# Dividing by the softmax denominators in the feed-forward, and another order of the attention's matmuls: layer 1 of a two-layer kernel

## Chip, cores and metric

The kernel runs on one core of a Trainium2 chip as one launch. The metric is the device time of that launch in microseconds (us). TensorE, VectorE (DVE), ScalarE (ACT), GpSimd (POOL) and SyncE (SP) have a queue each; SP issues the transfers between memory and the on-chip buffers. All data are float32. A matmul of high accuracy is made of three or two float32r passes over a "high" part and a "low" part (the remainder) of its operands.

## The reference, cut to what matters

Two layers over x of 4 x 1024 tokens by 512. Layer 1, which is changed here, is this:

```python
xn = _layernorm(x, axis=-1)
# attention: 16 heads of 32, sequences of 1024
q, k, v = (proj(wq), proj(wk), proj(wv))
q, k = apply_rope(q, k, sin, cos)
att = jnp.einsum('bhqd,bhkd->bhqk', q, k) * (1.0 / math.sqrt(HD))
att = jax.nn.softmax(att, axis=-1)
y = jnp.einsum('bhqk,bhkd->bhqd', att, v)
s = y.transpose(0, 2, 1, 3).reshape(b, t, c) @ wo.T
# feed-forward, hidden size 1408
g = _silu(_qlinear(_silu(_qlinear(xn, gate)) * _qlinear(xn, up), down))
x = x + s * g
```

## The kernel before

The program has four stages behind one another: layer 0's attention and feed-forward, then `layer1_attention` and `layer1_ffn`. Stages hand over through arrays in device memory: normalized x as transposed chunks of 128 tokens (`xt_chunks`, high and low part, 512 KB each), and the attention's y, transposed (`yt_chunks`).

**layer1_attention.** A pass (`tick`) handles one of 16 pairs of a batch and a group of four heads (`NT` = 16); 18 passes are run, the first two and last two unrolled, the 14 between in a loop of two passes per iteration. A pass has 16 steps and works on three group pairs at once. In pass t the steps prepare pair t (projections of its eight tiles of x, rope, transposes), find maxima for it and pair t-1, and make the attention of the second half of the queries of pair t-2 and the first half of t-1. The queues are ordered by hand:

- `scores`: for one tile of 128 keys and 512 queries, four passes of four matmuls (one per head, at different rows of the array) into `ps_sc`. The fourth subtracts the maxima, through `pick_max` and `max_t`. ScalarE then takes the exponentials (L1052); `ps_sc` is one buffer, so the next scores wait for them.
- `maximum`: two matmuls into `ps_max`, one buffer (L1188), and a reduction of it by VectorE (L1134). A step has two, the first called A and the second B below. `need(pe, max_read, ...)` makes each wait for the reduction of the one before.
- `pv`: the values, which multiply the probabilities of the step before into `ps_y` (L1198).
- `prepare`: one event. Odd steps: a projection (`proj`, L61, 12 matmuls), then rope on VectorE (L1118 to L1123), then copies by ScalarE. Even steps: a transpose of q and k (`turn`, L1216, with a high part by ScalarE and a low part by VectorE, L1128), a transpose of the maxima (`max`), or the sums over keys with a matrix of ones (`den`, L1228). All use `ps_prep`, one bank, so `released` makes each wait for the last one's reader.

The order on TensorE in a step is scores, maximum A, event, then in odd steps maximum B and values, and in even steps values and maximum B. VectorE's queue has in each step: reduction of A, rope (odd steps), reduction of B, low part (turns), and in eight steps of 16 a reciprocal of a quarter of the denominators (L1159). GpSimd adds the probabilities (L1101) and multiplies y by the reciprocals (L1107). SP loads x into two tiles and stores y:

```python
def tick(t, p):
    for c in range(CPB):
        if live(t, NT):
            ...
            need(sp, proj_done, CPB * t + c - 1)
            sp.dma_start(...xt[b]..., xt_in[src]).then_inc(xt_ld[b], 16)
    for qb in range(QB):
        if live(t - 2, NT):
            store(t - 2, qb)
```

**layer1_ffn.** One pass per chunk of 128 tokens, 32 chunks. TensorE: gate and up in three cuts of the hidden size (six groups into three banks `ps_gu`), transposes of the product of the chunk before, the attention's output projection with wo (`ps_s`), and the down projection of the chunk before. VectorE scales gate and up out of the banks (L1414, L1416) and makes low parts; ScalarE makes high parts (`yt_hi`, L1381) and silu; GpSimd multiplies gate and up.

Of the kernel before, what the change touches and what calls it, by code (L numbers as in the profile page):

```python
# [5 lines left out]
F32R = mybir.dt.float32r  # L6
# [841 lines left out]
def layer1_attention(nc, xt_in, wqkvT, rope_cos, rope_sin, yt_out):  # L848
# [11 lines left out]
    PIECES = 4  # L860
# [6 lines left out]
    with ExitStack() as ctx:  # L867
# [49 lines left out]
        xt = two("xt", [P, 2, KD, P], F32R)  # L917
# [9 lines left out]
        inv_den = sb("inv_den", [P, DIM])  # L927
        y_sb = two("y_sb", [P, DIM])
# [6 lines left out]
        xt_ld, y_stored = ([sem(f"{n}{i}") for i in range(2)] for n in ("xt_ld", "y_stored"))  # L935
# [5 lines left out]
        den_done, den_read, inverted = sem("den_done"), sem("den_read"), sem("inverted")  # L941
        y_copied, y_ready = sem("y_copied"), sem("y_ready")
# [67 lines left out]
        @block.sync  # L1010
        def _(sp):
            def tick(t, p):
                for c in range(CPB):
                    if live(t, NT):
                        b = c % 2
                        src = sp.snap(t // GROUPS * CPB + c) if not isinstance(t, int) else t // GROUPS * CPB + c
                        need(sp, proj_done, CPB * t + c - 1)
                        sp.dma_start(fp32(xt[b][:, :, :, :]).rearrange("p h k n -> p (h k n)"), xt_in[src]).then_inc(xt_ld[b], 16)
                for qb in range(QB):
                    if live(t - 2, NT):  # L1020
                        store(t - 2, qb)

            def store(m, qb):
                four = CPB // QB
                at = m // GROUPS * CPB + qb * four
                grp = m % GROUPS
                if not isinstance(m, int):
                    at, grp = sp.snap(at), sp.snap(grp)
                need(sp, y_ready, QB * m + qb + 1)
                sp.dma_start(yt_out[bass.ds(at, four), :, bass.ds(grp, 1), :].rearrange("c p a n -> p c (a n)"),  # L1030
                             y_sb[qb][:, :].rearrange("p (c n) -> p c n", n=P)).then_inc(y_stored[qb], 16)
            ticks(sp, *sched, tick)
            for b in range(2):
                sp.wait_ge(y_stored[b], 16 * NT)
# [128 lines left out]
        def _(pe):  # L1163
            head = lambda h: slice(HD * h, HD * h + HD)

            def scores(m, b, qb, kt):
# [3 lines left out]
                if kt == 0:  # L1170
                    need(pe, max_t_ready, QB * m + qb + 1)
# [347 lines left out]
```

## Time and profile before

| | us |
|---|---|
| median of the runs (3283.95 to 3290.11) | 3285.88 |
| the profiled execution | 3295.37 |
| its span | 3292.0 |
| TensorE busy in it | 2926.6 (89%) |
| VectorE | 1971.3 (60%) |
| GpSimd | 1324.0 (40%) |
| ScalarE | 1277.8 (39%) |
| mean granted TensorE clock | 0.949 of full speed |

The span is what the profile covers of one execution, from its first to its last instruction; the execution's own time is a little longer. A busy share is an average over four stages. Starts in a timeline are us from the span's start, and consecutive instructions of one kind are merged in one row (x4: four of them). The length of a matmul contains its way through the array, so matmuls follow one another more closely than their lengths say; the distance between two starts is what counts. A row of a timeline has the start, the length, engine, line, operation, what it writes and reads with shapes, and in brackets the idle time of its engine before it and what ended that. A row of the table by stretch has the stretch, its length, the busy time (and instructions) of TensorE's matmuls, its weight loads, VectorE, ScalarE and GpSimd, the granted TensorE clock as a share of full speed, the mean busy share of the DMA engines, and GB/s.

### The profile page before, as it was taken

What the parts mean: (1) busy time and instruction counts of PE and PEld (TensorE: products, weight loads), DVE (VectorE), ACT (ScalarE), POOL (GpSimd) and SP (SyncE); (2) the same over time, 40 slices, a digit from 0 to 9 for tenths busy, and PEclk for the clock granted to TensorE, in tenths of its full rate; (3) what the DMA queues carried; (4) which work ended last, traced back from release to release, by engine and by line L of the source; (5) the groups of instructions that cost most, each with busy time, mean ns of one, the idle gap of its engine ahead of it and who ended that gap; (6) DMA issues with size and microseconds to landing.
All of it is one profiled execution on the core that took longest, in us unless ns stands there. A gap on an engine that the chain in (4) does not pass through costs nothing. (4 is left out here: it accounts for less than half of the span.)

```text
span 3292.0 us, 56401 instructions
## 1 busy us (share of the span) xinstructions
PE 2926.6 (89%) x19876; PEld 2109.3 (64%) x19876; DVE 1971.3 (60%) x2924; ACT 1277.8 (39%) x1987; POOL 1324.0 (40%) x971
## 2 busy tenths in 40 slices
PE   5999999199999984799999999999999659999999
PEld 4888888078888873555555555555554248888887
DVE  4666665767777753676666666666666234444444
ACT  2111111066666651254544555455554412222222
POOL 1111010322333320377777777777777812112111
PEclk9999999599999996799999999999999979999999
DMA  2100000312222223111211111121111042212211
GB/s 83 33 32 32 32 32 20 118 52 96 96 90 82 99 74 113 52 54 63 65 59 59 64 58 59 58 65 58 59 59 33 13 184 74 70 64 72 72 64 51
DMA packets 97053, 215.00 MB, mean 65 GB/s; under 512 B 11408, under 2 KB 27792, under 8 KB 96400
## 3 DMA queue, kind: packets, MB, share of 16 engines
q1 hardware_dynamic: 95472, 210.14, 19.1%
q8 instruction: 115, 1.88, 0.2%
q10 hardware_dynamic: 1440, 2.76, 0.2%
q14 instruction: 26, 0.21, 0.0%
HBM read 162.54 MB, written 50.33 MB: 65 GB/s over the span
## 5 line engine op out<-in xcount | busy, mean ns | idle before, releaser
L1134 DVE TENSOR_REDUCE l_attn_maxima<-l_attn_ps_max 128x2 f32<-128x1024 f32 x512 | 618.6, 1208 | 229.7 <-PE l_attn_ps_max L1188 229.6
L1101 POOL TENSOR_TENSOR l_attn_summed<-l_attn_summed,l_attn_probs 128x1024 f32<-128x1024 f32 x256 | 600.4, 2379 | 132.6 <-ACT l_attn_probs L1052 132.5
L1052 ACT ACTIVATE l_attn_probs<-l_attn_ps_sc 128x1024 f32<-128x1024 f32 x512 | 496.7, 1022 | 274.1 <-PE l_attn_ps_sc L1177 271.5
L1101 POOL TENSOR_TENSOR l_attn_summed<-l_attn_probs 128x1024 f32<-128x1024 f32 x128 | 302.0, 2381 | 304.7 <-ACT l_attn_probs L1052 304.7
L70 PE MATMUL l_ffn_ps_gu<-l_ffn_w_gu,l_ffn_xt 128*128 128x512 f32 (+1 forms) x1536 | 345.0, 377 | 46.8 <-DMA l_ffn_xt<-xt_chunks 46.8
L61 PE MATMUL l_attn_ps_prep<-l_attn_wqkv_hi,l_attn_xt 128*128 (+1 forms) x1024 | 301.5, 378 | 74.7 <-DMA l_attn_xt<-xt_chunks 55.2
L70 PEld LDWEIGHTS l_ffn_ps_gu<-l_ffn_w_gu,l_ffn_xt 128*128 128x128 f32 x1536 | 279.1, 189 | 87.2 <-DMA l_ffn_xt<-xt_chunks 48.3
L1367 POOL TENSOR_TENSOR l_ffn_mixed<-l_ffn_gate,l_ffn_up 128x512 f32<-128x512 f32 (+1 forms) x96 | 115.1, 1199 | 521.8 <-DVE l_ffn_up L1416 473.5
L1188 PE MATMUL l_attn_ps_max<-l_attn_qk_hi 32*128 32x512 f32 x1024 | 252.6, 488 | 71.4 <-DVE l_attn_maxima L1134 71.3
L1188 PEld LDWEIGHTS l_attn_ps_max<-l_attn_qk_hi 32*128 32x128 f32 x1024 | 98.7, 189 | 281.7 <-DVE l_attn_maxima L1134 204.8
L1198 PE MATMUL l_attn_ps_y<-l_attn_probs,l_attn_v 128*32 128x512 f32 x2048 | 278.0, 616 | 1.1 <-ACT l_attn_probs L1052 1.1
L61 PEld LDWEIGHTS l_attn_ps_prep<-l_attn_wqkv_hi,l_attn_xt 128*128 128x128 f32 x1024 | 197.9, 208 | 112.4 <-issue 79.9
L70 PE MATMUL l_ffn_ps_fc<-l_ffn_t_fc,l_ffn_ct_hi 128*128 128x512 f32 x512 | 212.8, 416 | 7.0 <-DVE l_ffn_ct_lo L791 3.6
L1059 ACT ACTIVATE l_attn_x_tok<-l_attn_ps_prep 128x256 f32<-128x256 f32 x128 | 49.1, 383 | 414.3 <-DVE l_attn_ps_prep L1123 414.3
L70 PE MATMUL l_ffn_ps_out<-l_ffn_t_proj,l_ffn_ht_hi 128*128 128x512 f32 x512 | 203.9, 398 | 0.0
L70 PE MATMUL l_ffn_ps_fc<-l_ffn_t_fc,l_ffn_ct_lo 128*128 128x512 f32 x512 | 203.7, 398 | 0.0
L70 PE MATMUL l_ffn_ps_out<-l_ffn_t_proj,l_ffn_ht_lo 128*128 128x512 f32 x512 | 201.2, 393 | 0.0
L61 PE MATMUL l_attn_ps_prep<-l_attn_wqkv_lo,l_attn_xt 128*128 (+1 forms) x512 | 185.8, 363 | 0.0
L258 POOL TENSOR_TENSOR l_attn_rstd<-l_attn_mean_var,l_attn_ln_eps 128x1 f32<-128x1 f32 x32 | 6.1, 189 | 445.8 <-DVE l_attn_mean_var L325 445.8
L1177 PE MATMUL l_attn_ps_sc<-l_attn_qk_hi 32*128 32x512 f32 x1024 | 140.1, 491 | 22.7 <-ACT l_attn_probs L1052 12.3
L1118 DVE TENSOR_TENSOR l_attn_swapped<-l_attn_ps_prep,l_attn_sin_t 128x64 f32<-128x64 f32 x128 | 28.7, 225 | 205.9 <-PE l_attn_ps_prep L61 205.9
L1177 PEld LDWEIGHTS l_attn_ps_sc<-l_attn_qk_hi 32*128 32x128 f32 x1024 | 53.5, 184 | 150.8 <-issue 118.7
(235 smaller groups left out, 6215.1 us busy)
## 6 DMA issues: line engine op xcount, KB each, us to landing
l_attn_xt<-xt_chunks SPq DMA_DIRECT2D x128, 512.0 KB, 3.3
xt_chunks<-l_ffn_xt SPq DMA_DIRECT2D x32, 512.0 KB, 4.6
l_ffn_xt<-xt_chunks SPq DMA_DIRECT2D x32, 512.0 KB, 3.3
l_attn_xin<-in_x SPq DMA_DIRECT2D x32, 256.0 KB, 2.7
s<-l_attn_s_sb SPq DMA_DIRECT2D x32, 256.0 KB, 2.0
l_ffn_xa<-in_x SPq DMA_DIRECT2D x32, 256.0 KB, 2.7
l_ffn_xb<-in_x SPq DMA_DIRECT2D x32, 256.0 KB, 2.9
l_ffn_s_sb<-s SPq DMA_DIRECT2D x32, 256.0 KB, 4.0
```

The costliest lines, as they stand in the source:

```text
L61: mm = pe.matmul(out, a(k), w(k), start=(n == 0), stop=(n == 3 * slices - 1))
L70: mm = pe.matmul(out, a(k), w(k), start=(first and k == ks[0] and n == 0), stop=(last and k == ks[-1] and n == 1))
L258: pool.tensor_tensor(rstd[b][:, :], mean_var[b][:, 1:2], bn_eps[:, :], ALU.add).then_inc(rstd_ready, 1)
L1052: act.activation(probs[kt % RING][:, hs, :], ps_sc[:, hs, :], ACT.Exp, scale=ATT_SCALE).then_inc(exp_done, 1)
L1059: act.activation(x_tok[i % 4][:, :, :], ps_prep[:, 0:2, :], ACT.Copy)
L1101: pool.tensor_tensor(total[:, hs, :], old[:, hs, :], probs[kt % RING][:, hs, :], ALU.add).then_inc(added, 1)
L1118: dve.tensor_tensor(swapped[:, :, 0:R // 2], x[:, :, R // 2:R], tab(sin_t, 0, R // 2), ALU.mult).then_inc(rope_step, 1)
L1134: dve.tensor_reduce(maxima[b][:, j, PAIR * hp:PAIR * hp + PAIR, half:half + 1], ps_max[:, :, :], AX.X, ALU.max).then_inc(max_read, 1)
L1177: mm = pe.matmul(ps_sc[:, h, :], lhs, rhs, start=(k is qk_hi and q is qk_hi), stop=(k is None), skip_group_check=True)
L1188: mm = pe.matmul(ps_max[:, a, :], qk_hi[b][r, 0, P * j:P * j + P], qk_hi[b][r, 1, DIM * half:DIM * half + DIM], start=True, stop=True, ski ...
L1198: mm = pe.matmul(ps_y[head(h), :], v[b][:, kt, head(h)], probs[kt % RING][:, h, :], start=(kt == 0), stop=(kt == CPB - 1), skip_group_chec ...
L1367: pool.tensor_tensor(mixed[p][:, lo:hi], gate[p][:, lo:hi], up[p][:, lo:hi], ALU.mult).then_inc(mixed_ready, 1)
```

## The change

- Attention, TensorE: `scores` is split. A step is now: score passes 0 to 2, maximum A, pass 3, values, maximum B, event; the same in even and odd steps.
- Attention, x: four tiles in place of two. SP's loads are placed among four stores per pass.
- Attention, division: y and the denominators are copied by ScalarE and both stored (`den_chunks` is new). The reciprocals and the product leave this stage. VectorE's order is otherwise as it was.
- Feed-forward: it loads the denominators with y, two chunks ahead. VectorE takes four reciprocals per chunk, two behind each of cuts 1 and 2, and GpSimd multiplies. ScalarE's high part waits for that (`y_scaled`). The pass numbers of all engines begin at -2.

```diff
         def _(sp):
-            def tick(t, p):
-                for c in range(CPB):
...
-                        need(sp, proj_done, CPB * t + c - 1)
...
+            def load(m, c):
+                if live(m, NT):
+                    b = c % XTS
+                    src = m // GROUPS * CPB + c
+                    need(sp, proj_done, CPB * m + c - XTS + 1)
...
+            def tick(t, p):
+                load(t, 0)
+                store(t - 2, 0, y_copied, y_sb, yt_out)
+                load(t, 1)
+                load(t, 2)
+                load(t, 3)
+                store(t - 2, 0, den_read, den_sb, den_out)
+                load(t, 4)
+                load(t, 5)
+                load(t, 6)
+                store(t - 2, 1, y_copied, y_sb, yt_out)
+                load(t, 7)
+                store(t - 2, 1, den_read, den_sb, den_out)
...
-                            need(act, y_ready, QB * m + i)
-                            act.activation(inv_den[:, :], ps_prep[:, :, :].rearrange("p a n -> p (a n)"), ACT.Copy).then_inc(den_read, 1)
+                            need(act, y_den_stored[i], 32 * m)
+                            act.activation(den_sb[i][:, :], ps_prep[:, :, :].rearrange("p a n -> p (a n)"), ACT.Copy).then_inc(den_read, 1)
...
-                            pool.tensor_tensor(y_sb[qb][:, :], y_sb[qb][:, :], inv_den[:, :], ALU.mult).then_inc(y_ready, 1)
...
-                            dve.reciprocal(inv_den[:, cols], inv_den[:, cols]).then_inc(inverted, 1)
...
-            def scores(m, b, qb, kt):
+            def scores(m, b, qb, kt, passes):
...
-                for k, q in ((qk_hi, qk_hi), (qk_hi, qk_lo), (qk_lo, qk_hi), (None, None)):
+                for i in passes:
+                    k, q = ((qk_hi, qk_hi), (qk_hi, qk_lo), (qk_lo, qk_hi), (None, None))[i]
...
             def tick(t, p):
                 for s in range(STEPS):
...
                     if live(m, NT):
-                        scores(m, parity(p, 0 if s < CPB else 1), qb, kt)
+                        scores(*mine, (0, 1, 2))
                     if todo:
                         maximum(*todo[0])
-                    if event(t, s):
-                        prepare(t, p, s)
-                    if s % 2:
-                        for a in todo[1:]:
-                            maximum(*a)
+                    if live(m, NT):
+                        scores(*mine, (3,))
                     m, qb, kt = quad(t, s - 1) if s else quad(t - 1, STEPS - 1)
                     if live(m, NT):
                         pv(m, parity(p, 0 if s <= CPB else 1), qb, kt)
-                    if s % 2 == 0:
-                        for a in todo[1:]:
-                            maximum(*a)
+                    for a in todo[1:]:
+                        maximum(*a)
+                    if event(t, s):
+                        prepare(t, p, s)
...
-def layer1_ffn(nc, x1_in, xt_in, yt_in, woT, gateT, upT, downT, s_gate, s_up, s_down, out):
+def layer1_ffn(nc, x1_in, xt_in, yt_in, den_in, woT, gateT, upT, downT, s_gate, s_up, s_down, out):
...
-        sched = (-1, 4, CHUNKS - 2, CHUNKS + 1)
+        sched = (-2, 4, CHUNKS - 2, CHUNKS + 1)
...
+                    need(sp, y_scaled, c - 1)
+                    sp.dma_start(den[b][:, :, :], den_in[c]).then_inc(yt_den_ld[b], 16)
...
+                c, b = t + 2, p
+                if live(c, CHUNKS):
+                    need(pool, inverted, GROUPS * (c + 1))
+                    pool.tensor_tensor(yt[b][:, :, :], yt[b][:, :, :], den[b][:, :, :], ALU.mult).then_inc(y_scaled, 1)
...
-                    need(act, yt_ld[b], 8 * (c - b) + 16)
+                    need(act, y_scaled, c + 1)
...
+                    ci, bi = t + 2, p
+                    if live(ci, CHUNKS) and n:
+                        need(dve, yt_den_ld[bi], 16 * (ci - bi) + 32)
+                        for g in (2 * n - 2, 2 * n - 1):
+                            dve.reciprocal(den[bi][:, g, :], den[bi][:, g, :]).then_inc(inverted, 1)
```

## Rows read from the trace of the kernel before

**Rows 1.** Busy time by stretch: attention loop, its tail, feed-forward.

```profile
1399.60:2518.00 1118.40, 1023.96 (x8406) 571.91 (x8403) 763.11 (x1093) 569.72 (x813) 823.62 (x364) 0.97 0.19 60
2573.00:2611.00 38.00, 26.45 (x284) 10.37 (x284) 6.07 (x8) 23.54 (x26) 36.05 (x17) 1.00 0.03 8
2673.00:3292.00 619.00, 611.69 (x2976) 521.62 (x2976) 280.76 (x416) 165.28 (x289) 115.08 (x96) 1.00 0.20 67
```

**Rows 2.** TensorE's waits in the attention loop: us, times, longest.

```profile
PE l_attn_ps_max L1188 <- DVE l_attn_maxima L1134: 37.8, 112, 0.4
PE l_attn_ps_prep L61 <- DMA l_attn_xt<-xt_chunks: 34.2, 13, 4.3
PE l_attn_ps_prep L61 <- DVE l_attn_qk_lo L1128: 12.2, 43, 0.5
PE l_attn_ps_sc L1177 <- issue: 10.3, 6, 1.9
```

**Rows 3.** Timeline, an even and an odd step: start, length, engine, line.

```profile
2000.23 0.41 PE L1177 MATMUL l_attn_ps_sc<-l_attn_max_t,l_attn_pick_max 32*128 32x512 f32 x4
...
2000.80 0.66 PE L1216 MATMUL l_attn_ps_prep<-l_attn_ident,l_attn_x_tok 128*128 128x128 f32 x4
...
2002.38 0.50 PE L1188 MATMUL l_attn_ps_max<-l_attn_qk_hi 32*128 32x512 f32 x2
...
2002.68 0.50 PE L1177 MATMUL l_attn_ps_sc<-l_attn_qk_hi 32*128 32x512 f32 x4
...
2002.92 1.22 DVE L1134 TENSOR_REDUCE l_attn_maxima<-l_attn_ps_max 128x2 f32<-128x1024 f32 x1 [0.78 <-PE l_attn_ps_max L1188]
...
2004.20 0.50 PE L1188 MATMUL l_attn_ps_max<-l_attn_qk_hi 32*128 32x512 f32 x2 [0.31 <-DVE l_attn_maxima L1134]
...
2004.87 0.61 PE L61 MATMUL l_attn_ps_prep<-l_attn_wqkv_hi,l_attn_xt 128*128 x2 [0.18 <-DVE l_attn_qk_lo L1128]
...
2007.17 0.50 PE L1188 MATMUL l_attn_ps_max<-l_attn_qk_hi 32*128 32x512 f32 x2
...
2007.61 1.06 PE L1198 MATMUL l_attn_ps_y<-l_attn_probs,l_attn_v 128*32 128x512 f32 x8
...
2008.21 1.22 DVE L1134 TENSOR_REDUCE l_attn_maxima<-l_attn_ps_max 128x2 f32<-128x1024 f32 x1
...
2008.60 0.51 PE L1177 MATMUL l_attn_ps_sc<-l_attn_qk_hi 32*128 32x512 f32 x4
...
2009.40 0.42 PE L1177 MATMUL l_attn_ps_sc<-l_attn_max_t,l_attn_pick_max 32*128 32x512 f32 x4
...
2009.63 0.40 PE L1188 MATMUL l_attn_ps_max<-l_attn_qk_hi 32*128 32x512 f32 x2
...
2009.96 1.92 PE L1228 MATMUL l_attn_ps_prep<-l_attn_summed,l_attn_ones 128*32 128x512 f32 x16
...
2011.70 1.04 PE L1198 MATMUL l_attn_ps_y<-l_attn_probs,l_attn_v 128*32 128x512 f32 x8
```

**Rows 4.** Timeline of TensorE in pass 1, before there are scores.

```profile
1321.28 0.79 PE L1188 MATMUL l_attn_ps_max<-l_attn_qk_hi 32*128 32x512 f32 x2 [0.28 <-DVE l_attn_maxima L1134]
...
1323.49 0.79 PE L1188 MATMUL l_attn_ps_max<-l_attn_qk_hi 32*128 32x512 f32 x2 [1.41 <-DVE l_attn_maxima L1134]
```

**Rows 5.** Timeline of TensorE: three starts behind waits.

```profile
2038.59 0.67 PE L1177 MATMUL l_attn_ps_sc<-l_attn_qk_hi 32*128 32x512 f32 x4 [1.76 <-issue]
...
2524.68 0.50 PE L1188 MATMUL l_attn_ps_max<-l_attn_qk_hi 32*128 32x512 f32 x2 [1.32 <-DVE l_attn_maxima L1134]
...
2533.81 0.79 PE L1188 MATMUL l_attn_ps_max<-l_attn_qk_hi 32*128 32x512 f32 x2 [1.32 <-DVE l_attn_maxima L1134]
```

**Rows 6.** Timeline: end of the attention and start of the feed-forward.

```profile
2626.94 3.39 DVE L1159 RECIPROCAL l_attn_inv_den<-l_attn_inv_den 128x128 f32<-128x128 f32 x4 [25.81 <-ACT l_attn_inv_den L1072]
...
2630.47 1.26 POOL L1107 TENSOR_TENSOR l_attn_y_sb<-l_attn_y_sb,l_attn_inv_den 128x512 f32<-128x512 f32 x1 [6.54 <-DVE l_attn_inv_den L1159]
...
2678.41 0.68 DVE L1414 TENSOR_TENSOR l_ffn_gate<-l_ffn_ps_gu,l_ffn_sc_gu 128x512 f32<-128x512 f32 x1
```

More of the change, by code:

```diff
@@ L915, in _ @@
                     dve.tensor_tensor(w_lo[:, k, :, :], raw[:, k, :, :], fp32(w_hi[:, k, :, :]), ALU.subtract)
-        xt = two("xt", [P, 2, KD, P], F32R)
+        xt = [sb(f"xt{i}", [P, 2, KD, P], F32R) for i in range(XTS)]
         x_tok = [sb(f"x_tok{i}", [P, 2, P]) for i in range(4)]
@@ L933, in layer1_attention @@
         ps_y = ps("ps_y", [P, DIM])
-        xt_ld, y_stored = ([sem(f"{n}{i}") for i in range(2)] for n in ("xt_ld", "y_stored"))
+        xt_ld = [sem(f"xt_ld{i}") for i in range(XTS)]
+        y_den_stored = [sem(f"y_den_stored{i}") for i in range(QB)]
         proj_done, rope_step, proj_read = sem("proj_done"), sem("rope_step"), sem("proj_read")
@@ L1023, in store @@
[L1023 to L1031, printed above, removed]
+            def load(m, c):
[3 more added lines that the diff above has]
+                    need(sp, proj_done, CPB * m + c - XTS + 1)
+                    sp.dma_start(fp32(xt[b][:, :, :, :]).rearrange("p h k n -> p (h k n)"),
+                                 xt_in[src if isinstance(m, int) else sp.snap(src)]).then_inc(xt_ld[b], 16)
@@ new lines, in store @@
+            def store(m, qb, ready, tile, out):
+                if live(m, NT):
+                    four = CPB // QB
+                    at, grp = m // GROUPS * CPB + qb * four, m % GROUPS
+                    if not isinstance(m, int):
+                        at, grp = sp.snap(at), sp.snap(grp)
+                    need(sp, ready, QB * m + qb + 1)
+                    sp.dma_start(out[bass.ds(at, four), :, bass.ds(grp, 1), :].rearrange("c p a n -> p c (a n)"),
+                                 tile[qb][:, :].rearrange("p (c n) -> p c n", n=P)).then_inc(y_den_stored[qb], 16)
@@ L1176, in scores @@
                         lhs, rhs = (k[b][r, 1, keys], q[b][r, 0, queries]) if k else (pick_max[r, :], max_t[qb][r, :])
-                        mm = pe.matmul(ps_sc[:, h, :], lhs, rhs, start=(k is qk_hi and q is qk_hi), stop=(k is None), skip_group_check=True)
-                mm.then_inc(score_done, 1)
+                        mm = pe.matmul(ps_sc[:, h, :], lhs, rhs, start=(i == 0), stop=(i == 3), skip_group_check=True)
+                if passes[-1] == 3:
+                    mm.then_inc(score_done, 1)
             def maximum(m, b, i):
@@ L1326, in layer1_ffn @@
         ps_down = [ps(f"ps_down{i}", [P, DIM]) for i in range(2)]
-        xt_ld, yt_ld, x1_ld, stored = ([sem(f"{n}{i}") for i in range(2)] for n in ("xt_ld", "yt_ld", "x1_ld", "stored"))
+        xt_ld, yt_den_ld, x1_ld, stored = ([sem(f"{n}{i}") for i in range(2)] for n in ("xt_ld", "yt_den_ld", "x1_ld", "stored"))
+        inverted, y_scaled = sem("inverted"), sem("y_scaled")
         yt_hi_ready, yt_lo_ready = sem("yt_hi_ready"), sem("yt_lo_ready")
```

57 lines of the change are left out of this document (21 added, 36 removed).

## The prediction, made before the result was known

> **What bounds the kernel now.** I read the table of stretches first. Layer 1's attention loop (14 of its passes over one head group, two to a loop iteration) takes 1118.4 us of the 3292.0 us span, and TensorE is busy in 1023.96 of them; the feed-forward behind it is TensorE from end to end, 611.69 of 619 us [rows 1]. The list of TensorE's waits in the loop accounts for the missing 94.4 us: 37.8 us for the reading of the maxima (112 times, at most 0.4 us), 34.2 us for tiles of x (13 times, up to 4.3 us), 12.2 us for the low parts of q and k, and 10.3 us at the loop's six back edges [rows 2]. So a change of order can gain at most 37.8 + 34.2 + 12.2 = 84 us of idle time here, plus the slow matmuls that follow an x wait. VectorE is busy 763 of 1118 us, so it bounds nothing by its sum; but ps_max is one buffer, and every maximum waits until VectorE has read the last one. I then read the timeline of one even and one odd step.
>
> **The odd step.** Before, TensorE goes: scores, maximum A, projection, maximum B, values. VectorE's queue has: read A, rope (which waits for the projection), read B. After a projection ends, maximum B starts (2007.17), VectorE goes through rope and starts read B at 2008.21, done 1.22 later at 2009.43. In that time TensorE does the values (from 2007.61) and four score passes (2008.60 to 2009.40 from first to last start), and issues the next maximum at 2009.63: the rope and read B lie wholly beside 2.46 us of TensorE work [rows 3]. This cover is what the change takes away.
>
> **Part 1: the order on TensorE.** New, in every step: three score passes, maximum A, fourth pass, values, maximum B, and last the projection, turn, maxima's transpose or denominators. VectorE's queue keeps its order: rope still stands ahead of read B. So maximum B is now computed before the projection, and its reading still comes after projection and rope. Behind that reading stands maximum A of the next step, and behind that now also the fourth score pass, the exponentials and the values. Let T be the moment at which TensorE has issued the projection of an odd step:
> - Read B starts at T + 1.04, behind rope (2007.17 to 2008.21), and ends at T + 2.26. A maximum follows the end of a reading by 0.06 (reading 2002.92 + 1.22, maximum 2004.20 [rows 3]). Maximum A of the even step: T + 2.32. Three score passes are through at about T + 0.9 (0.80 to the start of the fourth), so TensorE now idles some 1.4 us.
> - From one maximum to the next with a free VectorE is 1.82 us: 2002.38 to 2004.20 [rows 3]. Between A and B lie the fourth pass, 0.23 (2009.40 to 2009.63), a change of shape, 0.33 (2009.63 to 2009.96), and the values, 0.99 (2007.61 to 2008.60), together 1.55, so the reading sets it: B at T + 4.14.
> - Between B and the next A lie 0.33, a turn of 0.66 and 0.80 of scores, 1.79, so again 1.82: A of the odd step at T + 5.96. The exponentials don't end later: from the fourth pass to the next scores is 2.45 (2000.23 to 2002.68), so they allow scores at T + 5.0 and A at T + 5.8.
> - B of the odd step: T + 7.78; change of shape 0.33; projection 2.30 (2004.87 to 2007.17). The next T is T + 10.41. I take 10.45, for a change of shape costs up to 0.44 (2007.17 to 2007.61).
>
> A pair with denominators has 1.74 us of them (2009.96 to 2011.70) between B and A: 0.33 + 1.74 + 0.80 = 2.87 in place of 1.82, so 11.50. The eight pairs of a pass (four turns, two maxima, two denominators) take 6 x 10.45 + 2 x 11.50 = 85.7 us, against 1118.4 / 14 = 79.9 before [rows 1]. The projection's 2.30, the rope's and reading's 2.3, and three cycles of 1.82 are now one chain with nothing beside it.
>
> **Part 2: four tiles of x, stores between the loads.** Before, the first tile of a pass is queued on SP behind the second y store, which waits for VectorE's reciprocals and GpSimd. After, tiles are requested up to four projections ahead. The store that precedes tile 1 waits for the copy of y in step 0, that before tile 4 for denominators of step 2, that before tile 7 for those of step 8; each tile then has over 10 us, where the longest wait for one was 4.3 [rows 2]. The 34.2 us and the half-rate matmuls behind them go. They are in the sum already, since 85.7 holds no x wait. At the back edges TensorE stops 1.7 us (10.3 / 6 [rows 2]). It overlaps rope and reading but delays the three score passes past T + 2.32, and they run slow there [rows 5]; VectorE has a back edge of its own in the chain, unseen, between 0 and the 1.8 of TensorE's. I take 2 us for each of six, 12 in all (bounds 6 and 24).
> Loop: 14 x 85.7 + 12 = 1212, against 1118.4: **+94** (bounds: 10.41 and no delay at the edges, +78; 0.1 more at each shape change and 24, +118).
>
> **Part 3: pass 1, which is unrolled.** Its second half has scores and loses like half a pass of the loop, 94 / 28 = 3.4, and a little at its start, where no x waits were to be had: +5. In its first half and the end of pass 0 there are only maxima and projections, and a maximum's two matmuls take 0.79 us instead of 0.50. There a cycle is 2.2 (1321.28 to 1323.49 [rows 4]); maximum B moved ahead of the projection adds one to each of seven odd steps, less some overlap: +13 (0 to 15). The last pass has maxima without projections in 11 steps; nothing is late there, and about 2 us of waits go: -2.
>
> **Part 4: the division.** In the attention it removes four reciprocals and one product per half. In the loop they lie in VectorE's and GpSimd's idle time, or delay the low parts (part of the 12.2 us), which 85.7 leaves out. At the end they are on the path: 2626.94 to 2631.73 [rows 6], and SP now stores the raw denominators there at 2626.9: -5, and -1 for a product out of GpSimd's last sums. The second store is another 32 transfers of 256 KB, beside the 0.19 DMA share of the stage [rows 1].
> In the feed-forward each chunk gets four reciprocals (3.39 us for four [rows 6]) on VectorE and a product of 1.26 us on GpSimd, two chunks ahead. VectorE is busy 281 of 619 us there [rows 1], so of 19.3 us per chunk 10.6 are free and 3.4 fit by their sum. Two reciprocals fall under the down projection; the other two, 1.7 us, delay the last scaling of gate and up, whose banks TensorE needs again only after 12 attention-output and 22 down matmuls. I cost the steady state at 0; uncovered it would be 32 x 1.7 = 54. At the start nothing covers. TensorE begins at 2673 [rows 1], and I put the landing of the first denominators 1 us behind; then for chunk 0 and again for chunk 1 come reciprocals 3.4, product 1.3 and some 1.3 for high and low part, before the first gate scaling, which so goes from 2678.4 [rows 6] to about 2687. TensorE's fourth group needs that bank, by an estimate from 24 matmuls, the first eight slow, at 2680: it waits 7 and starts slowly, +9 (0 to 12).
>
> **Sum.** 94 + 5 + 13 - 2 - 6 + 9 = **+113**. The profiled run took 3295.4 us with a span of 3292.0; the runs shown have a median of 3285.9, 0.3% less. On the median: 3285.9 + 113 = 3399, I say **3400 us**, slower by 3.5%. The forecast's own range, from the bounds (-16 and +24 in the loop, -13 in pass 1, -9 and +3 at the feed-forward's start, partly together), is 3365 to 3445.
>
> **The rule that weighs on it.** TensorE's clock fell to its lower level, 1.2 of 2.4 GHz, in some waits: at 2533.81, after 1.32 us of idle in a stretch with little else, a maximum lasts 0.79 instead of 0.50, while the same wait after full work left it at 0.50; scores behind a back edge of 1.76 took 0.67 against 0.51 [rows 3, 5]. At 70% busy (26.45 of 38 us) the granted clock stayed 1.00 [rows 1]. The new loop is 81% busy with one 1.4 us wait in 10.45, so I keep full rate. The Trainium skill ("TensorE: Matmul & The Clock Gate", section "HAM oscillation — how this bites in real kernels") says that waits between bursts can make every burst start at half rate. By that rule the sum would be that of rival B; by the rows it stays +113.
>
> **Rivals.**
> A. Faster (0.06). The reading of B does not hold TensorE, because its queue place costs less than I count. Then a turn pair is 8.96 (1.03 + 2.45 for the even step, the exponentials' bound; 0.95 + 1.82 + 0.4 + 2.3 for the odd), a pass 74, the loop 14 x 74 + 18 = 1054, the total about 3225. For it: 84 us of waits really go. Against: the place of rope in VectorE's queue, and 2.3 us measured behind it. It decides below (1118.4 - 12) / 112 = 9.88 us per pair, 0.84 less than the mean 10.72.
> B. The clock falls at each new 1.4 us wait (0.08). Two cycles of a pair go from 1.82 to 2.2 [rows 4], 0.76 x 112 = +85, so 3485; if the projection also runs at half rate, over 3600.
> C. The x waits stay (0.04): one of 4 us with slow matmuls, some 6 us, in seven iterations: 3440.
> D. The losses are smaller, since the matmuls behind a wait catch up (0.07): 3293 to 3365. Within 0.2%, about what a measurement can tell here, 0.03; this would need losses and gains to cancel.
> E. The forecast, 0.72.
> Range 3345 to 3465: it holds E but for its edges, C and part of D. Slower 0.91, same 0.03, faster 0.06.
>
> **What would show it.** In the changed profile: maximum A of even steps idle 1.3 to 1.5 us before it, released by VectorE's reading, 112 times in the loop, some 150 us in all; maximum starts 1.8 apart; a turn pair of 10.4 and a denominator pair of 11.5; no wait for x in the loop; granted clock at 0.97 or above in it; about 7 us of TensorE idle before the feed-forward's fourth group and a last attention store near 2627 plus the shift. Read B ahead of rope, or pairs under 9.9, would make it wrong.

## The result, and the profile after

The changed kernel takes 3567.7 us (median of four runs, 3565.8 to 3583.0), the kernel before 3288.0 in the same session: a ratio of 1.0859, 95% interval 1.0823 to 1.0895. It is slower by 8.6%; the forecast was 3.5% slower. The sign was right, and the loss is two and a half times as large as forecast. The profiled spans are 3563.0 and 3292.0 us, so 271 us have to be found.

Busy time by stretch for the changed kernel, the loop and the feed-forward: stretch, its length, busy time of TensorE, its weight loads, VectorE, ScalarE and GpSimd, granted clock, DMA share.

```profile
1410.26:2668.60 1258.34, 1087.42 (x8405) 551.71 (x8404) 683.40 (x980) 577.26 (x812) 791.20 (x337) 0.95 0.19 59
...
2810.20:3563.00 752.80, 661.47 (x2976) 548.20 (x2976) 377.84 (x544) 162.35 (x289) 155.79 (x128) 0.94 0.20 66
```

Against [rows 1] the same matmuls of the loop take 1258.3 us and not 1118.4, and those of the feed-forward 752.8 and not 619.0. The second row is the surprise: I had forecast 9 us there. To place the loss without gaps I cut the span at events that both traces have (the table is worked out from the start times of those instructions).

| stretch | before | after | difference | forecast |
|---|---|---|---|---|
| start to the first reading of a maximum in layer 1 | 1290.5 | 1280.6 | -9.9 | 0 |
| from there to the loop's first score pass | 109.1 | 129.7 | +20.6 | +18 |
| the loop | 1118.4 | 1258.3 | +139.9 | +94 |
| the loop's end to the last values | 96.9 | 89.6 | -7.3 | -2 |
| last values to the feed-forward's first matmul | 58.2 | 52.0 | -6.2 | -6 |
| from there to the first scaling of a down projection | 34.1 | 52.2 | +18.1 | +9 |
| first to last such scaling, 31 chunks | 579.5 | 695.3 | +115.8 | 0 |
| the rest | 5.3 | 5.3 | 0 | 0 |

The sum is 271.0. The first line is not the change's: those stages are the same in both, and among the kernels below the first reading comes anywhere from 1280.7 to 1290.5.

**The loop.** TensorE's waits in it (us, times, longest):

```profile
PE l_attn_ps_max L1189 <- DVE l_attn_maxima L1138: 147.2, 123, 1.3
PE l_attn_ps_sc L1177 <- issue: 6.9, 6, 1.5
```

The waits for x and for the low parts of [rows 2] are gone, and those for the maxima have gone from 37.8 to 147.2 us. The timeline shows two even steps, the first with denominators:

```profile
2007.29 1.22 DVE L1138 TENSOR_REDUCE l_attn_maxima<-l_attn_ps_max 128x2 f32<-128x1024 f32 x1
...
2008.56 0.50 PE L1189 MATMUL l_attn_ps_max<-l_attn_qk_hi 32*128 32x512 f32 x2 [1.33 <-DVE l_attn_maxima L1138]
...
2009.22 1.68 PE L1199 MATMUL l_attn_ps_y<-l_attn_probs,l_attn_v 128*32 128x512 f32 x8
2010.83 0.79 PE L1189 MATMUL l_attn_ps_max<-l_attn_qk_hi 32*128 32x512 f32 x2
2011.55 2.59 PE L1229 MATMUL l_attn_ps_prep<-l_attn_summed,l_attn_ones 128*32 128x512 f32 x16
...
2019.33 0.50 PE L1177 MATMUL l_attn_ps_sc<-l_attn_qk_hi 32*128 32x512 f32 x4
...
2020.37 1.22 DVE L1138 TENSOR_REDUCE l_attn_maxima<-l_attn_ps_max 128x2 f32<-128x1024 f32 x1
...
2021.64 0.50 PE L1189 MATMUL l_attn_ps_max<-l_attn_qk_hi 32*128 32x512 f32 x2 [1.33 <-DVE l_attn_maxima L1138]
...
2022.30 1.06 PE L1199 MATMUL l_attn_ps_y<-l_attn_probs,l_attn_v 128*32 128x512 f32 x8
2023.46 0.49 PE L1189 MATMUL l_attn_ps_max<-l_attn_qk_hi 32*128 32x512 f32 x2
2023.88 0.66 PE L1217 MATMUL l_attn_ps_prep<-l_attn_ident,l_attn_x_tok 128*128 128x128 f32 x4
2024.47 0.51 PE L1177 MATMUL l_attn_ps_sc<-l_attn_qk_hi 32*128 32x512 f32 x4
...
2029.84 0.50 PE L1177 MATMUL l_attn_ps_sc<-l_attn_qk_hi 32*128 32x512 f32 x4
```

Read the second step first. VectorE reads maximum B at 2020.37, behind the rope; TensorE has made three score passes and idles 1.33 us until that reading ends; from one first score pass (2019.33) to that of the next pair (2029.84) are 10.51 us. The forecast said 1.4 and 10.45. In the first step the same 1.33 us come before values of 1.68 in place of 1.06, a maximum of 0.79 in place of 0.49 and denominators of 2.59 in place of the 1.92 of [rows 3]: the clock fell behind the wait. The granted clock is 0.83 from 2005 to 2015 us and 1.00 from 2015 to 2025. Over the loop's 224 steps the medians are 5.15 us (turn or transpose of maxima), 6.41 (denominators) and 5.36 (projection), and 84 x 5.15 + 28 x 6.41 + 112 x 5.36 = 1212 us, where the forecast had 1200 (14 x 85.7) and 12 more for back edges. The other 46 us are what lies above the medians: 26 of 112 even steps are over 0.5 us longer than theirs, by 32 us in all, and 11 odd steps add the other 14; the trace has the granted clock at half in a part of every one of them. The back edges add next to nothing: most times the step before one is some 1.3 us longer and the next as much shorter, since its wait for the reading is gone.

**The feed-forward.** Waits from 2810 us on:

```profile
DVE l_ffn_den L1433 <- DMA l_ffn_den<-den_chunks: 199.1, 31, 8.3
...
PE l_ffn_ps_down L70 <- DVE l_ffn_ht_lo L1427: 73.5, 29, 2.8
...
PE l_ffn_ps_gu L70 <- DVE l_ffn_gate L1421: 10.6, 2, 7.8
```

Before, there were no waits of the first two kinds. The chunk period, from one scaling of a down projection to the next, is 695.3 / 31 = 22.43 us against 579.5 / 31 = 18.69. The timeline of one pass, SyncE's queue, VectorE and TensorE:

```profile
3103.09 0.69 DVE L1427 TENSOR_TENSOR l_ffn_ht_lo<-l_ffn_ps_turn,l_ffn_ht_hi 128x512 fp32r<-128x512 f32 x1 [0.38 <-ACT l_ffn_ht_hi L1397]
...
3105.39 0.33 SPq L1345 DMA_DIRECT2D l_ffn_xt<-xt_chunks  x1
...
3105.90 0.33 SPq L1347 DMA_DIRECT2D l_ffn_yt<-yt_chunks  x1
...
3106.36 0.34 SPq L1349 DMA_DIRECT2D l_ffn_den<-den_chunks  x1
...
3109.97 1.77 DVE L1433 RECIPROCAL l_ffn_den<-l_ffn_den 128x128 f32<-128x128 f32 x2 [6.19 <-DMA l_ffn_den<-den_chunks]
3111.65 0.63 DVE L1442 TENSOR_TENSOR l_ffn_res<-l_ffn_g_sb,l_ffn_x 128x512 f32<-128x512 f32 x1
3112.20 0.54 DVE L1421 TENSOR_TENSOR l_ffn_gate<-l_ffn_ps_gu,l_ffn_sc_gu 128x384 f32<-128x384 f32 x1
...
3113.71 0.56 DVE L1427 TENSOR_TENSOR l_ffn_ht_lo<-l_ffn_ps_turn,l_ffn_ht_hi 128x384 fp32r<-128x384 f32 x1 [0.50 <-ACT l_ffn_ht_hi L1397]
...
3114.32 0.50 PE L70 MATMUL l_ffn_ps_down<-l_ffn_w_down,l_ffn_ht_hi 128*128 128x512 f32 x1 [2.39 <-DVE l_ffn_ht_lo L1427]
...
3115.72 0.63 PE L70 MATMUL l_ffn_ps_down<-l_ffn_w_down,l_ffn_ht_lo 128*128 128x512 f32 x1
3116.14 5.12 PE L70 MATMUL l_ffn_ps_gu<-l_ffn_w_gu,l_ffn_xt 128*128 128x512 f32 x16
```

SyncE asks for the denominators at 3106.36, behind the load of x, which waits for all six gate and up groups of the pass. They land in front of 3109.97. VectorE has had their reciprocals at the head of its queue since 3103.78 (3103.09 + 0.69) and stands 6.19 us, with the residual sum, the scalings of cut 2 and its low part queued behind. TensorE goes through the attention output and most of the down projection, and then waits 2.39 us for that low part. The next 16 matmuls take 5.12 us; at full rate they take 3.79 (in e1 below). The wait of 2.39 and these 1.33 make 3.72 us, the whole of the longer period (22.43 - 18.69 = 3.74).

### The profile page after: what moved, and what is told of

Same layout as the page of the kernel before. It is cut to its first block and busy times, and to the rows that moved or that the text cites. A ratio compares the mean times of both kernels' runs of the same rounds, so it can differ in the third digit from the quotient of the medians.

```text
span 3563.0 us, 56561 instructions
## 1 busy us (share of the span) xinstructions
PE 3029.9 (85%) x19876; PEld 2105.0 (59%) x19876; DVE 1975.7 (55%) x2924; ACT 1283.3 (36%) x1987; POOL 1326.6 (37%) x971
## 5 line engine op out<-in xcount | busy, mean ns | idle before, releaser
L1189 PE MATMUL l_attn_ps_max<-l_attn_qk_hi 32*128 32x512 f32 x1024 | 265.8, 515 | 208.5 <-DVE l_attn_maxima L1138 189.5
L70 PE MATMUL l_ffn_ps_gu<-l_ffn_w_gu,l_ffn_xt 128*128 128x512 f32 (+1 forms) x1536 | 374.0, 399 | 52.2 <-DMA l_ffn_xt<-xt_chunks 41.6
L70 PEld LDWEIGHTS l_ffn_ps_gu<-l_ffn_w_gu,l_ffn_xt 128*128 128x128 f32 x1536 | 301.9, 204 | 103.5 <-DMA l_ffn_xt<-xt_chunks 43.3
L61 PE MATMUL l_attn_ps_prep<-l_attn_wqkv_hi,l_attn_xt 128*128 (+1 forms) x1024 | 287.1, 363 | 27.5 <-DMA l_attn_xt<-xt_chunks 21.3
L1199 PE MATMUL l_attn_ps_y<-l_attn_probs,l_attn_v 128*32 128x512 f32 x2048 | 292.7, 646 | 1.1 <-ACT l_attn_probs L1062 1.1
L1433 DVE RECIPROCAL l_ffn_den<-l_ffn_den 128x128 f32<-128x128 f32 x128 | 112.3, 921 | 199.1 <-DMA l_ffn_den<-den_chunks 199.1
L61 PEld LDWEIGHTS l_attn_ps_prep<-l_attn_wqkv_hi,l_attn_xt 128*128 128x128 f32 x1024 | 186.0, 196 | 60.3 <-issue 31.3
L1392 ACT ACTIVATE l_ffn_gate<-l_ffn_gate 128x512 f32<-128x512 f32 (+1 forms) x96 | 57.2, 596 | 425.5 <-DVE l_ffn_gate L1421 425.5
L70 PE MATMUL l_ffn_ps_down<-l_ffn_w_down,l_ffn_ht_hi 128*128 128x512 f32 x352 | 146.9, 417 | 73.5 <-DVE l_ffn_ht_lo L1427 73.5
L1177 PE MATMUL l_attn_ps_sc<-l_attn_max_t,l_attn_pick_max 32*128 32x512 f32 x1024 | 179.3, 438 | 0.0
```

The source lines that it names most:

```text
L61: mm = pe.matmul(out, a(k), w(k), start=(n == 0), stop=(n == 3 * slices - 1))
L70: mm = pe.matmul(out, a(k), w(k), start=(first and k == ks[0] and n == 0), stop=(last and k == ks[-1] and n == 1))
L1177: mm = pe.matmul(ps_sc[:, h, :], lhs, rhs, start=(i == 0), stop=(i == 3), skip_group_check=True)
L1189: mm = pe.matmul(ps_max[:, a, :], qk_hi[b][r, 0, P * j:P * j + P], qk_hi[b][r, 1, DIM * half:DIM * half + DIM], start=True, stop=True, ski ...
L1199: mm = pe.matmul(ps_y[head(h), :], v[b][:, kt, head(h)], probs[kt % RING][:, h, :], start=(kt == 0), stop=(kt == CPB - 1), skip_group_chec ...
L1392: act.activation(gate[p][:, lo:hi], gate[p][:, lo:hi], ACT.Silu).then_inc(silu_done, 1)
```

## The experiments

Ten kernels. For each I give the ratio to the kernel before, timed beside it (medians of 3290.7 to 3292.0 us there), and two numbers of its one trace: the attention's length, from the first reading of a maximum to the last values, and the feed-forward's chunk period.

| kernel | median us | ratio, 95% interval | attention us | chunk us |
|---|---|---|---|---|
| before | 3288.0 | 1 | 1324.4 | 18.69 |
| changed | 3567.7 | 1.0859 (1.0823 to 1.0895) | 1477.6 | 22.43 |
| e1 early loads | 3431.3 | 1.0428 (1.0409 to 1.0448) | 1456.3 | 18.69 |
| e2 old order, early loads | 3229.6 | 0.9813 (0.9793 to 0.9834) | 1267.2 | 18.69 |
| e3 read first | 3337.8 | 1.0135 (1.0113 to 1.0157) | 1237.5 | 22.51 |
| e4 filler | 3531.3 | 1.0725 (1.0703 to 1.0747) | 1435.4 | 22.53 |
| e5 read first, early loads | 3202.9 | 0.9730 (0.9707 to 0.9754) | 1238.0 | 18.69 |
| e6 order alone | 3478.3 | 1.0574 (1.0543 to 1.0605) | 1515.3 | 18.69 |
| e7 four x tiles | 3374.9 | 1.0255 (1.0228 to 1.0282) | 1410.0 | 18.69 |
| e8 division kept | 3345.5 | 1.0162 (1.0136 to 1.0187) | 1391.6 | 18.69 |
| e9 four x tiles, mended | 3233.4 | 0.9833 (0.9803 to 0.9863) | 1265.9 | 18.69 |
| e10 division kept, mended | 3264.8 | 0.9927 (0.9905 to 0.9950) | 1297.4 | 18.69 |

**e1: the loads of the feed-forward earlier.** On the changed kernel:

```diff
                 if live(c, CHUNKS):
-                    need(sp, gu_done, 2 * N * (c - 1))
-                    sp.dma_start(fp32(xt[b]...), xt_in[c]).then_inc(xt_ld[b], 16)
                     need(sp, yt_lo_ready, c - 1)
                     sp.dma_start(yt[b][:, :, :], yt_in[c]).then_inc(yt_den_ld[b], 16)
                     need(sp, y_scaled, c - 1)
                     sp.dma_start(den[b][:, :, :], den_in[c]).then_inc(yt_den_ld[b], 16)
+                    need(sp, gu_done, 2 * N * (c - 1))
+                    sp.dma_start(fp32(xt[b]...), xt_in[c]).then_inc(xt_ld[b], 16)
```

> The changed kernel, with SyncE's loads of y and of the denominators of chunk t+2 issued ahead of the load of x (which waits for the gate and up groups of pass t), everything else kept. Theory 1, the late load: the denominators land in mid pass, VectorE stands at the reciprocals for some 6 us with the work of cut 2 queued behind them, and the down projection waits; with the loads a pass ahead the chunk period goes from 23.2 us back to 19.1 to 19.6, so the whole falls from 3568 to some 3430 to 3450 us, and VectorE's waits for the denominators (199 us in 31) go. Rival, the reciprocals' own work: their 2 x 1.7 us in VectorE's queue in front of cut 2 delay it by themselves: then 32 x 1.7 = 54 us of the loss stay and the whole is about 3490, or with both pairs exposed 3545.

It took 3431.3 us, 136 less than the changed kernel, and the chunk period is 18.69, that of the kernel before. The same place of its timeline:

```profile
3109.51 1.75 DVE L1433 RECIPROCAL l_ffn_den<-l_ffn_den 128x128 f32<-128x128 f32 x2
3111.18 0.63 DVE L1442 TENSOR_TENSOR l_ffn_res<-l_ffn_g_sb,l_ffn_x 128x512 f32<-128x512 f32 x1
...
3111.23 0.33 SPq L1349 DMA_DIRECT2D l_ffn_xt<-xt_chunks  x1
...
3113.72 1.76 DVE L1433 RECIPROCAL l_ffn_den<-l_ffn_den 128x128 f32<-128x128 f32 x2
3113.72 0.42 SPq L1347 DMA_DIRECT2D l_ffn_den<-den_chunks  x1
...
3118.96 3.79 PE L70 MATMUL l_ffn_ps_gu<-l_ffn_w_gu,l_ffn_xt 128*128 128x512 f32 x16
```

The reciprocals do the same work in the same place, and nothing waits in front of them; the load at 3113.72 is for the pass after. So the late load was all of the steady loss, and the reciprocals' own 3.5 us per chunk cost nothing. The wait for the gate scaling at the start of the stage went from 10.6 to 3.3 us, since the first denominators no longer stand behind x either. Of the 144.6 us between the two profiled spans, 116 are the period, 11 the start of the stage, and 21 attention whose code is the same in both (1456.3 against 1477.6), less 4 ahead of it: how often the clock falls there differs between the two (16 of 112 even steps are over 0.5 us longer here, 26 there).

**e2: the old order on TensorE as well.** All four score passes, maximum A, the event, maximum B ahead of the values in odd steps and behind them in even ones, as in the kernel before.

> As the run before it, and TensorE's order in the attention put back (all four score passes, maximum A, the event, then maximum B before the values in odd steps and behind them in even ones); four x tiles, denominators stored beside y and the division in the feed-forward stay. Theory 1, the order is the attention's whole loss: the loop goes from 1258 us to 1118 less the x waits of 34 to 43 us, the feed-forward is at its old pace, and the whole is 3230 to 3275 us, faster than the kernel before (3288). Rival, the loss in the attention comes from what else is new there (twice the stores, the copy of the denominators, SyncE's queue): the loop stays over 1180 and the whole over 3330.

3229.6 us, just below the lower edge of the interval: faster than the kernel before by 1.9%. The attention takes 1267.2, that is 189 us less than with the change's order (e1) and 57 less than before. Twice the stores and the copy of the denominators cost nothing that shows: e9 below, without them, takes 1265.9.

**e3: VectorE reads maximum B ahead of the rope.** On the changed kernel:

```diff
-                    if e and e[0] == "proj":
-                        rope(e[1], e[2])
                     for a in todo[1:]:
                         maximum(*a)
+                    if e and e[0] == "proj":
+                        rope(e[1], e[2])
```

> The changed kernel with one swap on VectorE in odd steps: the read of maximum B ahead of the rope instead of behind it; the feed-forward is as changed. Theory 1, the chain: the read of B stands behind the rope, which waits for the projection, and so maximum A of the next step waits 1.34 us and the clock falls behind some of these waits; the pair goes from 10.5 us to 9.0 to 9.6, the clock stays full, the loop goes from 1258 to 1060 to 1110 us and the whole from 3568 to some 3370 to 3420. Rival, the wait only moves: the rope then ends later, the copy and the turn behind it too, and TensorE waits there: the loop stays over 1200 and the whole over 3510.

3337.8 us, below even the favourable end: 230 us from one swap. Its list of waits in the loop and its timeline:

```profile
PE l_attn_ps_max L1189 <- DVE l_attn_maxima L1138: 4.5, 14, 0.3
```

```profile
2010.13 0.50 PE L1177 MATMUL l_attn_ps_sc<-l_attn_qk_hi 32*128 32x512 f32 x4
...
2013.21 1.22 DVE L1138 TENSOR_REDUCE l_attn_maxima<-l_attn_ps_max 128x2 f32<-128x1024 f32 x1 [0.60 <-PE l_attn_ps_max L1189]
2015.39 0.51 PE L1177 MATMUL l_attn_ps_sc<-l_attn_qk_hi 32*128 32x512 f32 x4
...
2016.22 0.30 DVE L1127 TENSOR_TENSOR l_attn_ps_prep<-l_attn_ps_prep,l_attn_swapped 128x128 f32<-128x128 f32 x1
...
2018.99 0.50 PE L1177 MATMUL l_attn_ps_sc<-l_attn_qk_hi 32*128 32x512 f32 x4
```

The reading of B (2013.21) lies beside the projection and the rope (its last part at 2016.22) beside the next scores. Odd step 5.26, even step 3.60, a pair of 8.9 in place of 10.5; a denominator step takes 4.8 in place of 6.4; the granted clock from 1450 to 2350 us is 1.00. The rival, that the wait moves to the turn behind a later rope, found nothing: the list of waits is empty but for 4.5 us and the back edges.

**e4: more work in the wait.** The changed kernel with the first score pass made twice in even steps:

```diff
                     if live(m, NT):
-                        scores(*mine, (0, 1, 2))
+                        scores(*mine, (0, 1, 2) if s % 2 else (0, 0, 1, 2))
```

> The changed kernel with the first of the three score passes made twice in even steps (four more matmuls of 0.21 us, 0.85 us a step, in front of maximum A, where TensorE waits 1.34 us for VectorE; the values are the same). Theory 1, the clock: the full-rate loop would be 7 x 172.8 = 1210 us and the other 48 us are steps at half rate begun by these waits; with the wait filled to 0.5 us the pairs keep their 10.5 us, the clock stays full, and more work takes less time: the loop is about 1210 us and the whole 3510 to 3530. Rival, the half-rate steps have another cause: the loop stays at 1258 and the whole at 3568. If the 1.34 us are not slack, the added work costs 112 x 0.85 = 95 us and the whole is 3660.

3531.3 us: 36 less with 448 matmuls more in the loop. The same 1200 us of the changed kernel and of this one:

```profile
1410.00:2610.00 1200.00, 1036.96 (x8016) 525.41 (x8015) 652.57 (x937) 550.20 (x775) 752.24 (x320) 0.95 0.19 61
```

```profile
1410.00:2610.00 1200.00, 1051.36 (x8753) 548.94 (x8750) 675.30 (x969) 571.95 (x805) 784.00 (x334) 1.00 0.20 62
```

The granted clock is 1.00 in place of 0.95, and more gets done on every engine (805 instructions of ScalarE against 775). The pairs keep their 10.5 us. One number of my expectation was wrong, as the timeline of this kernel shows:

```profile
2016.04 0.74 PE L1177 MATMUL l_attn_ps_sc<-l_attn_qk_hi 32*128 32x512 f32 x8
...
2018.34 0.50 PE L1189 MATMUL l_attn_ps_max<-l_attn_qk_hi 32*128 32x512 f32 x2 [1.10 <-DVE l_attn_maxima L1138]
```

Eight of these matmuls take 0.74 where four take 0.50, so the added pass filled 0.24 us of the wait, not 0.85, and the wait is still 1.10. [Rows 3] could have told: there the first to the fourth score pass are 0.80 us apart, 0.27 for a pass of four. The Trainium skill ("TensorE: Matmul & The Clock Gate", "Part 3: Packing small matmuls — row/col tiling") says that matmuls on 32 rows each, in different row groups, run side by side; these do. The experiment shows that the 46 us are half-rate time that goes with these waits: with more matmuls in them the loop takes 1213.3 us, and the granted clock is full in every step. It doesn't show whether the shorter wait or the added work does it, nor where between 1.10 and 1.34 us the difference arises.

**e5: both mends.**

> Both mends at once on the changed kernel: the read of maximum B ahead of the rope, and the loads of y and of the denominators ahead of the load of x. Theory: the two losses are apart (the one is in the attention's loop, the other in the feed-forward), so the savings add up: 3338 less 3.74 us for each of 31 chunks and some 12 us at the feed-forward's start is 3205 us, faster than the kernel before by 2.5%. Rival, the stages share something (the clock, the DMA engines): the savings overlap by 30 us or more and the whole is over 3235.

3202.9 us: the two losses are apart and add up, and this is the fastest version, 2.7% faster than the kernel before and 10% faster than the changed one, with all three parts of the change in it.

**e6: the change's order alone, on the kernel before.**

> The kernel before with the change's order on TensorE alone (maximum A between the third score pass and the last, the values next, then maximum B, then the event); two x tiles, SyncE's order and the division stay where they were. Theory 1, the order is the loss of the attention: the pair goes to 10.5 us and the clock falls in part, the loop from 1118 to 1210 to 1280 us, and the whole is 3390 to 3450. Rival, the order is only bad together with the copies and stores of the denominators: the whole is below 3340.

3478.3 us. The rival falls, but the interval was 28 us too low: the attention takes 1515.3 us, 38 more than in the changed kernel. Two things are in the attention here that the changed kernel has moved or mended: the division, which costs something under this order (e10 shows it without the clock's part), and the two tiles of x, whose waits are small (4.9 us in 1000 us of the loop). How the 38 us divide between these and the clock is not shown.

**e7 and e8: four x tiles without the moved division.** e7 is the kernel before with four tiles; e8 has the change's order and the read of B first as well. In both I put the y stores between the loads:

```diff
+                for c in range(4):
+                    load(c)
+                if live(t - 2, NT):
+                    store(t - 2, 0)
+                for c in range(4, CPB):
+                    load(c)
+                if live(t - 2, NT):
+                    store(t - 2, 1)
```

> The kernel before with four tiles of x and its loads four projections ahead, the store of y behind the fourth and the eighth of them; nothing else. Theory 1: the waits for x (34 us in the loop, some 43 in all) go, the clock behind them stays full, and the whole is 3230 to 3255. Rival, the waits are hidden anyway or move to the maxima: the whole is 3275 or more. Against the run with the old order and the division in the feed-forward (3230) it also shows what the moved division is worth once its loads are early: theory 0 to 20 us.

> The kernel before with four tiles of x, the change's order on TensorE and the read of maximum B ahead of the rope, but with the division kept in the attention (VectorE's reciprocals in pieces of 0.86 us, eight of 16 steps, and GpSimd's product). Theory 1, the move of the division matters here: at a pair of 8.9 us VectorE's reciprocals come between the reads of maxima, and the loop is 10 to 60 us longer than with the division moved: the whole is 3215 to 3260 against some 3205. Rival, VectorE has room for them: the whole is within 8 us of the run with both mends.

Both missed by over 80 us: 3374.9 and 3345.5. Waits of TensorE and of SyncE's queue in e7, 1000 us of the loop, and its timeline:

```profile
PE l_attn_ps_prep L61 <- DMA l_attn_xt<-xt_chunks: 82.3, 23, 5.0
```

```profile
SPq L1037 <- POOL l_attn_y_sb L1114: 921.0, 23, 42.6
```

```profile
1998.92 1.28 POOL L1114 TENSOR_TENSOR l_attn_y_sb<-l_attn_y_sb,l_attn_inv_den 128x512 f32<-128x512 f32 x1
2000.43 0.41 SPq L1037 DMA_DIRECT2D yt_chunks<-l_attn_y_sb  x1
2001.19 2.06 SPq L1020 DMA_DIRECT2D l_attn_xt<-xt_chunks  x4
...
2005.30 1.00 PE L61 MATMUL l_attn_ps_prep<-l_attn_wqkv_hi,l_attn_xt 128*128 x2 [3.98 <-DMA l_attn_xt<-xt_chunks]
```

With the division in the attention, the product that a store waits for is made at the end of step 7 and of step 15. Four loads stood behind that store and went out together at 2001.19. The kernel before has one such wait for x in a pass (13 in 14 passes of the loop [rows 2]), behind its second store; e7 has two (23 in 1000 us), since its first store stands ahead of loads as well. So four tiles were worse than two. e8 has the same 23 waits for x, 50.6 us of TensorE, and beside them 60.6 us of waits for the maxima.

**e9 and e10: the same two with SyncE's queue mended.** Each store now goes where its product is ready when the queue reaches it:

```diff
-                if live(t - 2, NT):
-                    store(t - 2, 0)
+                if live(t - 3, NT):
+                    store(t - 3, 1)
                 for c in range(4, CPB):
                     load(c)
                 if live(t - 2, NT):
-                    store(t - 2, 1)
+                    store(t - 2, 0)
```

> The kernel before with four tiles of x, and SyncE's stores of y put where they never stand unready in front of a load: the second store of a head group goes behind the fourth load of the next pass, the first behind the eighth load (in the run with four tiles before, they waited 921 us for GpSimd's product in SyncE's queue with loads behind them, and TensorE waited 82 us for x). Theory 1: that queue was the whole loss of that run; the waits for x are under 5 us and the whole is 3230 to 3255. Rival, the four tiles or the crowding of loads cost by themselves: the whole stays over 3290.

> As the run with the division kept in the attention, the change's order on TensorE and the read of maximum B first, with the same mend of SyncE's queue. Against the run with both mends of the changed kernel (3203) only the place of the division differs. Theory 1, VectorE's reciprocals (0.86 us in eight of 16 steps) stand between the reads of maxima, as the 60.6 us of TensorE's waits for maxima in the unmended run say: the waits for x go, those for the maxima stay, and the whole is 3245 to 3275. Rival, the waits for the maxima came from the late x too: the whole is within 8 us of 3203, and moving the division is worth nothing.

Both hit. e9 takes 3233.4 us: the x waits are gone, and four tiles alone, well queued, are worth 1.7%. Beside e2 (3229.6) it also says that under the old order the place of the division is worth nothing in the attention (1265.9 and 1267.2 us). Under the new order, with B read first, it is worth 59 us: 1297.4 in e10, 1238.0 in e5. With the division kept, the new order is even 31 us slower than the old (1297.4 against 1265.9): it gains only together with the moved division. TensorE's waits in e10 for the maxima, 1000 us of the loop, and one place of its timeline:

```profile
PE l_attn_ps_max L1199 <- DVE l_attn_maxima L1142: 66.7, 102, 1.1
```

```profile
1890.07 1.22 DVE L1142 TENSOR_REDUCE l_attn_maxima<-l_attn_ps_max 128x2 f32<-128x1024 f32 x1 [0.60 <-PE l_attn_ps_max L1199]
...
1891.35 0.50 PE L1199 MATMUL l_attn_ps_max<-l_attn_qk_hi 32*128 32x512 f32 x2
...
1892.13 0.94 DVE L1167 RECIPROCAL l_attn_inv_den<-l_attn_inv_den 128x128 f32<-128x128 f32 x1
...
1892.99 1.16 DVE L1142 TENSOR_REDUCE l_attn_maxima<-l_attn_ps_max 128x2 f32<-128x1024 f32 x1
...
1894.21 0.50 PE L1199 MATMUL l_attn_ps_max<-l_attn_qk_hi 32*128 32x512 f32 x2 [1.13 <-DVE l_attn_maxima L1142]
```

The maximum of 1891.35 is read only at 1892.99, since VectorE's queue has the low part of the turn and then a reciprocal of 0.94 us between the two readings, and TensorE waits 1.13 us for that reading. The two kernels' steps differ in their medians around the reciprocals alone, by 0.5 us in even and up to 0.9 in odd ones, 4.2 us in a pass of the loop.

## Why the prediction was wrong

**The step that failed** is in Part 4: "so of 19.3 us per chunk 10.6 are free and 3.4 fit by their sum", and from it "I cost the steady state at 0". It measured 116 us. Of the 158 us by which the spans' difference (271) exceeds the forecast (113), that is the largest part; the clock in the attention's loop, below, is 46 more, and the other stretches nearly cancel. The sum was right: the reciprocals fit, as e1 shows. What I left out is when their input is there. The load is the third in SyncE's queue behind a wait for the pass's last gate and up group, it lands 4.6 us after SyncE is let go (3105.39 to 3109.97), and its reader stands in VectorE's in-order queue ahead of the work of cut 2. Of that work I counted only the scaling, whose banks TensorE needs late; behind it stands the low part that the down projection of the same pass needs. All of this stands in the diff and in the kernel before: where each load waits, how long a load of this size takes, and what is queued behind its first reader. I did ask that question for the first chunks only ("I put the landing of the first denominators 1 us behind"). That I priced the uncovered case at 54 us, from the length of the reciprocals, shows the same blind spot: VectorE's 6.2 us are set by the load's landing, and the 3.7 us a chunk by what of them reaches TensorE (2.39) and by the clock behind it (1.33).

**Part 1, the order: right in mechanism and in its full-rate size.** Wait 1.33 (1.4), pair 10.51 (10.45), medians that add up to 1212 us (1200; a denominator pair is 11.67 and not 11.50). The 12 us for the back edges did not come, so the two misses cancel. e3 confirms the place, VectorE's queue with the rope ahead of reading B, and e2 that without the order nothing of the attention's loss is left.

**The clock: a term of the sum that was mis-sized.** "The new loop is 81% busy with one 1.4 us wait in 10.45, so I keep full rate" measured +46 us. I gave rival B 0.08 for a fall at each wait (+85); it came at about a quarter of them. Of the two rows that I had for a wait of 1.32 us, one showed the clock fall and one did not [rows 5]: they bore out a partial case, which should have been in the forecast. The Trainium skill ("TensorE: Matmul & The Clock Gate", section "HAM oscillation — how this bites in real kernels"), which I had weighed, states that waits between bursts let the clock fall, each time in its example, where they are longer (some 3 to 5 us). The trace agrees in kind with waits of 1.33 us, but only in 26 of 112 even steps.

**Part 2: right.** No wait for x is left. e9 puts it at 58 us in the attention when done alone (1324.4 to 1265.9), more than the 34.2 us of waits; the half-rate matmuls behind them go too (granted clock in the loop 0.97 before [rows 1], 1.00 in e9). e7 shows what it hangs on: where the stores stand in the queue.

**Part 3: right**, +20.6 (18), and -7.3 for -2 at the end. **The end of the attention:** -6.2 for -6. **The start of the feed-forward:** +18.1 for +9; the forecast wait of 7 us is there (7.8, and another of 2.8), with the first denominators read 3 us behind TensorE's start and not 1, and the first passes have the late load too.

**Rival A**, the faster one, was priced at 8.96 a pair and a total of 3225. The kernel that has it, e3 and with early loads e5, runs at 8.9 and 3202.9. The price was right within 1%; what it needs is the read ahead of the rope, and the prediction named that as what would overturn it.

Shown by runs: the late load (e1), the rope ahead of reading B (e3), the order as the whole of the attention's loss (e2), the clock's share (e4). Open: why the clock falls behind some of these waits and not behind others of equal length. Not run: the old order with B read first, so how much of the 29 us between e2 and e5 is the order's and how much the swap's is not shown.

## What to carry to other kernels

When work is moved to another stage, ask for each new input when its load is issued, what that load waits for, and what stands behind its first reader on an in-order engine. Free time on the engine answers none of these: here 3.5 us of work with room to spare cost 3.7 us a chunk until its load went ahead of one that waits. When one order is changed, look at the other engine's order beside it: reordering TensorE alone lost 189 us, and with VectorE's one pair of operations swapped to match, the two together gained 29 over the old orders (e5 against e2 in the attention), but only where the division had left VectorE's queue. And a store that waits for its data holds up every load behind it: four tiles of x lost 86 us or won 58 in the attention by nothing but where the stores stood (e7, e9).

## What I had not expected of the hardware

- In waits of equal length, 1.34 us once a pair, the clock fell behind about a quarter (26 of 112 even steps; 16 of 112 in e1's trace of the same code). With the wait cut to 1.10 us by four more matmuls the granted clock was 1.00 over 1200 us, against 0.95.
- The same attention code took 1477.6 and 1456.3 us in two executions (changed kernel and e1), with a granted clock of 0.95 and 0.97 from 1450 to 2350 us. Almost without waits (e3, e5) it was 1237.5 and 1238.0. Two traces of each are too few to say that such waits make a loop repeat less well.
- Four more matmuls on 32 rows each, in four row groups, cost 0.24 us together, as much as one of the feed-forward's matmuls on all rows (3.79 us for 16, in e1).
